# Attention value products issued in bursts of three steps instead of one step at a time

## The reference

```python
q = jnp.einsum('bsd,hdk->bhsk', x, wq)
k = jnp.einsum('bsd,hdk->bhsk', x, wk)
v = jnp.einsum('bsd,hdk->bhsk', x, wv)
scores = jnp.einsum('bhsk,bhtk->bhst', q, k) / jnp.sqrt(jnp.asarray(K, x.dtype))
probs = jax.nn.softmax(scores, axis=-1)
o = jnp.einsum('bhst,bhtk->bhsk', probs, v)
```

## Time and profile before

| | |
|---|---|
| median of 3 runs | 5213.08 us |
| profiled execution, first to last instruction | 5214.6 us |
| of it before the first step, all engines | 119.4 us |
| first item, an item of the loop, last item, rest | 253.2 us, about 319 us, 286.6 us, 97.3 us |
| PE busy | 4965.0 us, 95% |
| DVE, POOL, ACT busy | 73%, 54%, 51% |
| TensorE clock granted, mean | 0.980 |

### The profile page before, as it was taken

One profiled execution on the slowest core, in us unless ns is written; L12 is line 12 of the kernel. 1 busy time (PEld: TensorE's weight loads), 2 busy tenths in 40 slices (PEclk: granted clock), 3 DMA queues, 4 the chain that ended last, 5 costly groups with the idle time before them and its releaser, 6 DMA issues. The chain is left out here.

```text
span 5214.6 us, 92843 instructions
## 1 busy us (share of the span) xinstructions
PE 4965.0 (95%) x25829; PEld 3227.2 (62%) x25829; DVE 3832.6 (73%) x8495; ACT 2665.8 (51%) x6408; POOL 2796.0 (54%) x1611
## 2 busy tenths in 40 slices
PE   5999999999999999999999999999999999999997
PEld 3556666666566666666666666666666656666666
DVE  5667768677776777777777776777867777677765
ACT  2664555555544545545455455455455554554542
POOL 0665555555555555555555555555555555555652
PEclk7999999999999999999999999999999999999998
DMA  1000000000000000000000000000000000000000
GB/s 39 6 10 7 6 16 6 11 7 6 16 6 10 7 10 11 6 11 11 10 6 6 10 11 11 7 6 16 6 11 7 6 16 6 10 6 10 6 1 14
DMA packets 43025, 49.54 MB, mean 10 GB/s; under 512 B 26256, under 2 KB 34311, under 8 KB 42503
## 3 DMA queue, kind: packets, MB, share of 16 engines
q1 hardware_dynamic: 42503, 43.12, 2.7%
HBM read 23.45 MB, written 19.09 MB: 8 GB/s over the span
## 5 line engine op out<-in xcount | busy, mean ns | idle before, releaser
L1155 POOL TENSOR_TENSOR sums<-sums,probs 128x736 f32<-128x736 f32 (+3 forms) x1344 | 2384.6, 1774 | 1278.0 <-ACT probs L867 1262.6
L867 ACT ACTIVATE probs<-scores 128x368 f32<-128x368 f32 (+3 forms) x3456 | 1460.1, 474 | 1922.0 <-PE scores L761 1814.5
L925 DVE TENSOR_REDUCE part_max<-work 128x1 f32<-128x368 f32 (+3 forms) x3456 | 1657.3, 527 | 310.1 <-PE work L675 288.3
L778 PE MATMUL o_ps<-probs,values 128*64 128x368 f32 (+1 forms) x6912 | 1455.7, 500 | 0.0
L759 PE MATMUL scores<-q_a,k_a 128*128 128x368 f32 (+3 forms) x3456 | 1170.2, 339 | 61.1 <-issue 41.5
L761 PE MATMUL scores<-q_b,k_b 128*128 128x368 f32 (+3 forms) x3456 | 1146.4, 332 | 0.0
L675 PE MATMUL work<-k_a,q_a 128*128 128x368 f32 (+3 forms) x3456 | 1089.6, 378 | 48.0 <-DVE part_max L925 24.4
L675 PEld LDWEIGHTS work<-k_a,q_a 128*128 128x128 f32 (+1 forms) x3456 | 578.3, 184 | 777.4 <-issue 624.1
L1151 POOL TENSOR_TENSOR sums<-probs 128x736 f32<-128x736 f32 (+1 forms) x192 | 343.6, 1789 | 863.5 <-ACT probs L867 861.5
L759 PEld LDWEIGHTS scores<-q_a,k_a 128*128 128x128 f32 (+1 forms) x3456 | 639.5, 185 | 83.8 <-issue 33.2
L761 PEld LDWEIGHTS scores<-q_b,k_b 128*128 128x128 f32 (+1 forms) x3456 | 641.3, 186 | 53.0 <-issue 33.7
(11 more groups left out here) (186 smaller groups left out, 5039.6 us busy)
## 6 DMA issues: line engine op xcount, KB each, us to landing
resid_rows<-h_in SPq DMA_DIRECT2D x16, 576.0 KB, 2.8
h_out<-resid_rows SPq DMA_DIRECT2D x16, 576.0 KB, 4.1
h_in<-in_pe_table_dram SPq DMA_DIRECT2D x16, 512.0 KB
out_dram<-h_out SPq DMA_DIRECT2D x16, 512.0 KB
q_b<-max_rows SPq DMA_DIRECT2D x128, 4.0 KB
q_b<-max_rows SPq DMA_DIRECT2D x128, 0.3 KB
counts<-in_x_dram SPq DMA_DIRECT2D x16, 116.0 KB, 3.0
out_raw<-n_expert_out_weight_dram SPq DMA_DIRECT2D x1, 1024.0 KB
```

The costliest lines, as they stand in the source:

```text
L778: mm = nc.tensor.matmul(o_ps[64 * i:64 * i + 64, 0:cw], values[0:n, t, h * DH:(h + 1) * DH], probs[0:n, s % NP, i, 0:cw], start=(t == 0), ...
L867: nc.scalar.activation(probs[0:n, s % NP, i, 0:cw], scores[0:n, h % SB, 0:cw], ACT.Exp, scale=DH ** -0.5).then_inc(probs_ready, 1)
L925: nc.vector.tensor_reduce(part_max[0:n, i * NT + j, c:c + 1], w[0:n, 0:keys], AX.X, ALU.max).then_inc(drained[k], 1)
L1155: nc.gpsimd.tensor_tensor(acc, acc, probs[0:n, s % NP, :, 0:cw], ALU.add).then_inc(sums_done, 1)
```

## The change

`weigh` is now called only in steps whose number divides by three, for the three steps before (`GROUP` = 3): 12 PE instructions stand one behind the other where there were three times 4. In the two steps between, PE issues only scores and units. What else goes with it:

- `probs` has 5 buffers: the last step of a group always uses buffer 4, the first two use buffers 0 and 1 or 2 and 3 in turn (`slot`). ACT may therefore be 6 steps ahead for the first two and 3 for the last (`held`).
- ACT copies `o_ps` out one step later (tile 1 of the next chunk instead of tile 0), since the last products of a chunk come a step later.
- the `sum` unit of a chunk moves from 2 steps behind its end to 3, which is a burst step.
- `plan` books 66 for a step's scores on PE, and 240 on every third step for the burst, where it booked 130 for every step. So `v` and expert units go elsewhere: mostly out of the burst steps.
- for room in SBUF `h_in`, the input rows of the next item, lies over the part of `heads_t` that holds the fourth pair's outputs, and `beats` over `logits`. SP waits for the last `proj` unit before it loads `h_in`, ACT waits for the store of `h_in` before it writes the fourth pair's first output.

```diff
-NP = 3
+NP = 5
+GROUP = 3
...
-STEP = (130, 0, 70)
+SCORE = (66, 0, 70)
+WEIGH = (240, 0, 0)
...
-    used = [list(STEP) if attn else [0, 0, 0] for _ in range(ALL)]
+    used = [list(SCORE) if attn else [0, 0, 0] for _ in range(ALL)]
+    for s in range(0, ALL, GROUP):
+        if attn:
+            used[s] = [a + w for a, w in zip(used[s], WEIGH)]
...
-            put(NT * (q + 1) + 2, ("sum", q))
+            put(NT * (q + 1) + 3, ("sum", q))
...
-    h_in = sb(ctx, "h_in", [P, NT, D])
+    h_in = heads_t[:, (PAIRS - 1) * TP:].rearrange("p (a n) -> p a n", a=NT)
...
+    def slot(s):
+
+        return s // GROUP % 2 * 2 + s % GROUP if s % GROUP < GROUP - 1 else NP - 1
+
+    def held(s):
+
+        return GROUP if s % GROUP == GROUP - 1 else 2 * GROUP
...
+        def weigh(seg, it, b, s):
+
+            for done in range(s - GROUP, s):
+                weigh_one(seg, it, b, done)
...
-                weigh(seg, it, b - 1, ALL - 1)
-            if seg.attn and s > 0:
-
-                early = len(units) // 2 if s % NT else 0
+                weigh(seg, it, b - 1, ALL)
+            if seg.attn and s > 0 and s % GROUP == 0:
+
+                early = len(units) // 2
                 for u in units[:early]:
                     unit(seg, it, b, u)
                 units = units[early:]
-                weigh(seg, it, b, s - 1)
+                weigh(seg, it, b, s)
...
-                wait(act, probs_used, ALL * b + s - NP + 1)
-                if not isinstance(b, int) or b > 0 or s >= NP:
-                    wait(act, sums_done, (NT - 1) * PAIRS * NC * b + summed(s - NP))
+                back = held(s)
+                wait(act, probs_used, ALL * b + s - back + 1)
+                if not isinstance(b, int) or b > 0 or s >= back:
+                    wait(act, sums_done, (NT - 1) * PAIRS * NC * b + summed(s - back))
...
-                if t == 0 and s > 0:
+                if t == 1 and s > 1:
                     heads(seg, it, b, s // NT - 1)
```

More of the change, by code:

```diff
@@ L512, in fusion_kernel @@
     sums = sb(ctx, "sums", [P, 2, 2, CHUNK])
-    heads_t = sb(ctx, "heads_t", [P, PAIRS, TW])
+    heads_t = sb(ctx, "heads_t", [P, (PAIRS - 1) * TP + TW])
     part_max = sb(ctx, "part_max", [P, 2 * NT, NC])
@@ L543, in fusion_kernel @@
     rank = sb(ctx, "rank", [P, NT, EG])
-    beats = sb(ctx, "beats", [P, 3, NT, 3])
+    beats = logits[:].rearrange("p a n -> p (a n)")[:, 0:9 * NT].rearrange("p (d a n) -> p d a n", d=3, a=NT)
     four = sb(ctx, "four", [P, EG])
@@ L694, in unit @@
                 for p in range(PAIRS):
-                    mm = nc.tensor.matmul(w[:, 0:D], heads_t[:, p, j * P:(j + 1) * P], wo[:, p, :],
+                    mm = nc.tensor.matmul(w[:, 0:D], heads_t[:, p * TP + j * P:p * TP + (j + 1) * P], wo[:, p, :],
                                           start=(p == 0), stop=(p == PAIRS - 1))
@@ L762, in score, with weigh_one @@
                                  start=False, stop=True).then_inc(scores_ready, 1)
-        def weigh(seg, it, b, s):
+        def weigh_one(seg, it, b, s):
             p, c, t = cut(s)
@@ L778, in weigh @@
                 mm = nc.tensor.matmul(o_ps[64 * i:64 * i + 64, 0:cw], values[0:n, t, h * DH:(h + 1) * DH],
-                                      probs[0:n, s % NP, i, 0:cw], start=(t == 0), stop=(t == NT - 1))
+                                      probs[0:n, slot(s), i, 0:cw], start=(t == 0), stop=(t == NT - 1))
             mm.then_inc(probs_used, 1)
+        def weigh(seg, it, b, s):
+            for done in range(s - GROUP, s):
+                weigh_one(seg, it, b, done)
         def step(seg, it, b, s):
@@ L853, in heads @@
                 wait_filled(act, seg, it, ("proj", 3 * q + 2))
+            if q == (PAIRS - 1) * NC and seg.prep:
+                act.wait_ge(resid_stored, 16 * (b + 2))
             c0, cw = CHUNKS[q % NC]
-            nc.scalar.copy(heads_t[:, q // NC, c0:c0 + cw], o_ps[:, 0:cw]).then_inc(heads_out, 1)
+            nc.scalar.copy(heads_t[:, q // NC * TP + c0:q // NC * TP + c0 + cw], o_ps[:, 0:cw]).then_inc(heads_out, 1)
         def step(seg, it, b, s):
@@ L866, in step @@
                     act.wait_ge(scores_ready, 2 * ALL * b + h + 1)
-                    nc.scalar.activation(probs[0:n, s % NP, i, 0:cw], scores[0:n, h % SB, 0:cw], ACT.Exp,
+                    nc.scalar.activation(probs[0:n, slot(s), i, 0:cw], scores[0:n, h % SB, 0:cw], ACT.Exp,
                                          scale=DH ** -0.5).then_inc(probs_ready, 1)
-                if t == 0 and s > 0:
+                if t == 1 and s > 1:
                     heads(seg, it, b, s // NT - 1)
-            if s == 0 and seg.ends:
+            if s == 1 and seg.ends:
                 heads(seg, it, b - 1, PAIRS * NC - 1)
@@ L1150, in step @@
                     pool.wait_ge(heads_scaled, PAIRS * NC * b + q - 1)
-                nc.gpsimd.tensor_tensor(acc, probs[:, (s - 1) % NP, :, 0:cw], probs[:, s % NP, :, 0:cw],
+                nc.gpsimd.tensor_tensor(acc, probs[:, slot(s - 1), :, 0:cw], probs[:, slot(s), :, 0:cw],
                                         ALU.add).then_inc(sums_done, 1)
@@ L1154, in step @@
                 pool.wait_ge(sums_done, (NT - 1) * (PAIRS * NC * b + q) + t - 1)
-                nc.gpsimd.tensor_tensor(acc, acc, probs[0:n, s % NP, :, 0:cw], ALU.add).then_inc(sums_done, 1)
+                nc.gpsimd.tensor_tensor(acc, acc, probs[0:n, slot(s), :, 0:cw], ALU.add).then_inc(sums_done, 1)
         for r in range(2):
@@ L1188, in step @@
                 wait_then(wait, sp, norm_ready[0], NT * (b + 1))
+                if seg.post:
+                    wait_then(wait_drained, sp, seg, it, ("proj", NT - 1))
                 seed(b + 1)
```

5 lines of the change are left out of this document (2 added, 3 removed).

## The result

The changed kernel took 5292.8 us (median of 4 runs, 5290.1 to 5311.9) against 5213.5 us of the kernel before: 1.0159 times as long, with a 95% interval of 1.0141 to 1.0177. It is 79 us slower where 273 us less was forecast.

What follows compares the result with a forecast made beforehand. PE was taken as the bound almost everywhere, by how long its instructions stand apart. 5214.6 - 385 (joins) + 84 (ACT) + 27 (DVE) = 4941 us profiled, 4939 at the median, said as 4940; range 4860 to 5055.

Steps and rivals of the forecast that it cites:

- A join is worth 0.35 us, 385 us in all: PE's value products: joining one step's to others saves 0.35 us; 1089 fewer stretches of 64-row matmuls give 385 us.
- Rival C: Inside a burst: the array restarts for each step, 115 us, giving 5055; chance 0.04 (joining does nothing, 5213: 0.02).
- DVE's term: Groups with maxima: DVE sets the pace where busy longer than PE's shortened group, 1.69 us an item, 27 us over 16.
- ACT's term: Projection groups, steps 0 to 5 of a pair: no gain at all in 126 groups, 84 of the 385 us given up.
- cover the burst itself: The four `work` banks: a late DVE has up to four reductions waiting, about as long as the burst lasts.
- The upper bound for DVE, 270 us: Groups with maxima: if every group lost as much as the worst, 0.6 x 450 = 270 us.
- ACT waits 1.4 us behind the burst in a projection group, a loss of up to 0.65 us a group: Burst step: after its exponentials ACT waits for the projection behind the burst; a group takes 10.3 us against 9.69.
- Buffers, overlay, copy of the outputs a step later: nothing: Five `probs` buffers, SP's and ACT's new waits, later copy of `o_ps`: all costed at nothing.
- The sum unit a step later: slack: End of a chunk: the `sum` unit's moved wait is over earlier relative to its producer; costed at nothing.
- The end of an item, 0 to 22 us: Transfer of the maxima before the next scores: just covered, taken as nothing; at worst 1.5 us in each of 15 items.
- Rival B: ACT and DVE take most: projection groups lose 0.65 us each (+82), DVE twice its term (+27); 5050, 5010 to 5120; chance 0.17.
- the clock, D: Projection groups: ACT's wait stops PE so long that its clock falls to 0.50, making it slower than before; chance 0.02.

## Why the prediction was wrong, point by point

*A join is worth 0.35 us, 385 us in all.* Right in the timeline: 2.00 us for twelve products, 1.30 us around one step. Over 241 stretches of twelve in the changed kernel that stand between matmuls of 368 columns, the way from the matmul before to the second one behind is 2.54 us at the lower quartile, against 1.30 + 2 x 0.615 = 2.53. Rival C is refuted by the same rows.

*ACT takes back 84 us, DVE 27.* **This is the step that failed.** From 5214.6 - 385 to the measured 5291.7 are 462 us, not 111. The larger miss is DVE's term. In the 84 steps an item without projections it was to take back 1.7 us; these steps took back 18.6 (19.8 by count less the 1.2 measured), some 298 us over 16 items, and shorter maxima return 11.4 of them. ACT's term stood for projection groups that gain nothing; they lost 7.2 us an item. The working compared busy times of three steps, and took DVE's mean of 6.63 of 8.85 us for the low end. But what had to be compared is what each engine can do between two points of its order. One of its own rows spoke against it: in the stretch of 13.25 us PE was busy for only 10.45 and DVE for 12.75, so DVE set the pace there already, and taking PE's 0.67 us off it was no valid step. The half-sentence that the four banks "cover the burst itself" is the one that the fifth bank contradicts: it is worth 136 us with bursts and 49 before. The rows show why for projections: their bank is held until ACT and DVE have both been there, each behind older work. The upper bound for DVE, 270 us, would have been near; with the upper bound for ACT (+82 us) in place of no gain, the sum gives 5266. The measured time is above that too.

*ACT waits 1.4 us behind the burst in a projection group, a loss of up to 0.65 us a group.* The mechanism is right: 2.14 us of idle time in the rows above, and the projection steps return to their old length when all units, the projection among them, go ahead of the burst. The size was above the upper bound: the three stretches lost 1.49, 1.67 and 2.04 us, for two groups each, and the loop's mean is 0.9 us a group. Going back to single steps there did shorten these steps, but not the kernel.

*The two short steps between bursts.* The prediction did not have them. It asked what the burst step does to ACT and DVE, and not what PE does in the steps that lost their value products. By the price of the earlier trace rows it arrives at the next units 0.97 us earlier in each. In the stretch shown that is while ACT and DVE are late; how often it is so elsewhere was not counted.

*Buffers, overlay, copy of the outputs a step later: nothing.* Right for buffers and overlay: undone bursts and the moved sums alone run within 4 us of each other (5251.6 and 5255.2). *The sum unit a step later: slack.* Wrong for the kernel before (42 us), and wrong in its reason: not the sum's own wait counts, but the stretches that it no longer shares (17 us) and, as far as the waits tell, the places of the maxima. In the changed kernel it costs nothing.

*The end of an item, 0 to 22 us.* At step 27 the transfer of the maxima is now waited for (0.80 us in the item shown). In total PE waits 13.5 us for it (first line), 5.8 before (second line), both in the whole execution:

```profile
PE scores L772 <- DMA q_b<-max_rows: 13.5, 14, 4.1
PE scores L759 <- DMA q_b<-max_rows: 5.8, 2, 4.1
```

*Rival B and the clock, D.* B had the mechanism, and 5010 to 5120 for it. The clock had a share. One of its falls in the changed kernel, the stretch before and the stretch of it:

```profile
2487.10:2490.50 3.40, 1.05 (x8) 0.93 (x8) 2.62 (x4) 3.32 (x9) 2.26 (x2) 1.00 0.00 0
2490.50:2493.90 3.40, 3.40 (x11) 2.65 (x9) 3.17 (x7) 0.77 (x3) 0.65 (x1) 0.50 0.02 5
```

PE was busy for 1.05 of 3.4 us, and then ran at 1.2 GHz. In the first stretch ACT was busy for 3.32 us and DVE for 2.62. The mean granted clock of the whole execution fell from 0.980 to 0.968. As lost clock that is 0.032 x 5291.7 - 0.020 x 5214.6 = 65 us at most; part of it lies in time when PE had nothing to do. Stretches at a granted 0.50 grew from 28 to 56 in the whole execution, and from 213 to 339 us together. In the fall shown the stop comes first and the lower clock makes it dearer. So D was part of the loss, though most of the 462 us lies outside it. The Trainium skill's warning in "TensorEngine Tiling (Array Packing)", section "PSUM Bottleneck", that the emptying of PSUM may become the bottleneck once TensorE is sped up, is what the table of shortened maxima shows here, with DVE at only 71%.

What stays open: with DVE and ACT shortened, the bursts bring 132 us of their 385, so 253 us are still taken back. By steps this is 9.7 us an item in the projection steps (4.2 by count and 5.5 lost) and 7.1 in the others (19.8 less 12.7). How each of the two divides between the projections' chain, the experts' chain, the clock and the banks is not shown; of these only the banks and the units' place ahead of the burst were tested.

## What to carry to other kernels

When an order by hand is changed to save time on the busiest engine, ask for each other in-order engine what work lies ahead of it at the point where the busy engine turns away from it, and how late it is when that engine comes back; a mean of 71% can hide that it is late where it counts. Count a buffer that passes through two engines as held until the second is done: here the fifth bank was worth 136 us. And test a suspected co-limiter by the same relief in both kernels: the difference of differences tells what it takes back, which waits of 30 to 70 us each did not. Then split the time by kinds of steps as well: a total that hardly moves (44 us here) can hide a cure in one kind and a loss in another.

## What the runs showed of the hardware

Matmuls of 64 output rows for two heads start in pairs, and a pair in the middle of such a stretch takes about 0.31 us, the stretch's entry and exit together about 0.35 us more. That held for stretches of 4, 8 and 12 instructions, with program waits between them, and for 16 in the kernels with joined sums.

I had not expected that DVE operations whose operands lie all in SBUF differ so much in length while POOL works. The first line below is two additions of POOL; they stand in the trace from 2747.34 to 2749.10 and from 2749.18 to 2750.93.

```profile
2747.34 3.60 POOL L1175 TENSOR_TENSOR sums<-sums,probs 128x736 f32<-128x736 f32 x2 [1.98 <-ACT probs L888]
2748.83 0.49 DVE L1023 CAST flat_hi<-normed 128x384 fp32r<-128x384 f32 x1
2749.35 2.00 DVE L1024 TENSOR_TENSOR flat_lo<-normed,flat_hi 128x384 fp32r<-128x384 f32 x1
```

Both DVE operations began during an addition and ended shortly after it, the first 0.22 and the second 0.42 us later. That is so throughout the changed kernel. In 30 of its 48 executions L1024 began while POOL was adding; all 30 ended 0.41 to 0.42 us after that addition, wherever in it they had begun (median 1.99 us long). The other 18 took 0.56 us. L1023 behaved the same in 29 of 48 (end 0.21 to 0.22 us after the addition, 0.35 us long otherwise). The maxima (L946), which read PSUM, took 0.53 us in the median with or without POOL at work. By these rows the two operations waited for the end of POOL's addition; what this costs the kernel was not tried.
